# Relation features of each unit made inside the next unit of the expert mixture, in 64-row products of three passes

## The reference

```python
# layer 0, the mixture (8 experts, each with its batch norm _bn):
    h = jax.nn.relu(_bn(jnp.einsum('bfd,edh->bfeh', x, W1) + b1, g1, be1, m1, v1))
    h = jax.nn.relu(_bn(jnp.einsum('bfeh,ehk->bfek', h, W2) + b2, g2, be2, m2, v2))
    y = jnp.einsum('bfeh,ehd->bfed', h, Wo) + bo
    return jnp.einsum('bfed,fe->bfd', y, softmax(feat @ Wr + br))
# layer 1: xn = _layernorm(x), message (u->v) in relation r: norm_e * xn[u], then blockwise
    W = weight.reshape(R, NUM_BASES, SUBMAT_IN, SUBMAT_OUT)       # 8 relations, 8 blocks of 32x32
    out = jnp.einsum('rnbi,rbio->nbo', agg, W)
```

## Time and profile before

| | us |
|---|---|
| median of three runs | 7881.05 |
| the profiled execution | 7916.16 |
| its span | 7914.4 |
| TensorE busy | 5702.7 (72%) |
| VectorE busy | 4775.0 (60%) |
| ScalarE busy | 3998.3 (51%) |
| GpSimd busy | 3494.5 (44%) |

### The profile page before, as it was taken

How to read it: one execution, slowest core, us unless ns; L and a number is a source line. 1 busy time by engine, 2 the same in 40 slices (tenths; PEclk the granted TensorE clock), 3 DMA queues, 4 the chain that set the end, 5 groups by cost and what they waited for, 6 DMA issues and landing times. The chain is left out here.

```text
span 7914.4 us, 97807 instructions
## 1 busy us (share of the span) xinstructions
PE 5702.7 (72%) x22256; PEld 4016.0 (51%) x22256; DVE 4775.0 (60%) x13022; ACT 3998.3 (51%) x13304; POOL 3494.5 (44%) x3571
## 2 busy tenths in 40 slices
PE   3567777755677777547777777999987666666688
PEld 2434444434455555335555445888854555445445
DVE  5545555566555555855665557888843555656584
ACT  4456666665667766747677665444453111111032
POOL 2455566525656665266666660000002545556501
PEclk8767788776788888768888888999998777777799
DMA  5434444335333333343333333555575223222212
GB/s 164 124 104 111 111 118 113 110 89 151 100 98 104 102 100 98 108 137 101 101 103 100 100 99 119 200 188 192 192 238 194 85 86 90 85 81 80 71 41 66
DMA packets 511972, 920.50 MB, mean 116 GB/s; under 512 B 89659, under 2 KB 345611, under 8 KB 511435
## 3 DMA queue, kind: packets, MB, share of 16 engines
q0 software_dynamic: 166320, 446.82, 20.7%
q1 hardware_dynamic: 345259, 469.88, 18.4%
HBM read 773.29 MB, written 152.30 MB: 117 GB/s over the span
## 5 line engine op out<-in xcount | busy, mean ns | idle before, releaser
L1863 POOL DMA_INDIRECT gm_got<-scratch_feat,keep_src_tab x2490 | 2376.2, 954 | 1519.8 <-PE gm_bank L2141 678.1
L2141 PE MATMUL gm_bank<-gm_got,gm_onehot 128*128 128x264 f32 x4980 | 1886.2, 484 | 1013.9 <-DVE gat_acc L2023 482.6
L2085 ACT ACTIVATE gm_got<-gm_got 128x64 f32<-128x64 f32 x9804 | 2427.8, 334 | 271.4 <-issue 206.6
L2141 PEld LDWEIGHTS gm_bank<-gm_got,gm_onehot 128*128 128x128 f32 x4980 | 971.1, 226 | 1643.8 <-issue 793.5
L2023 DVE TENSOR_TENSOR gat_acc<-gat_acc,gm_bank 128x264 f32 x2490 | 1060.6, 426 | 1129.1 <-PE gm_bank L2141 512.1
L1151 POOL DMA_INDIRECT mix1a_got<-scratch_rel_feat,layer_rel_tab x240 | 238.9, 996 | 1483.6 <-issue 1359.0
L1151 POOL DMA_INDIRECT mix1b_got<-scratch_rel_feat,layer_rel_tab x590 | 588.3, 997 | 461.2 <-PE mix1b_m_bank L1208 234.0
L1208 PE MATMUL mix1b_m_bank<-mix1b_got,mix1b_onehot 128*128 128x256 f32 x1180 | 417.1, 498 | 311.3 <-DVE logit_acc L1182 249.4
L1208 PEld LDWEIGHTS mix1b_m_bank<-mix1b_got,mix1b_onehot 128*128 128x128 f32 x1180 | 269.4, 246 | 426.2 <-DVE mix1b_onehot L1160 213.2
L2030 DVE TENSOR_TENSOR gm_onehot<-gm_iota,keep_dst_tab 128x640 f32<-128x640 f32 x498 | 404.4, 812 | 73.9 <-issue 50.7
L850 POOL DMA_INDIRECT scratch_first<-gat_scores,keep_first_pos x150 | 200.8, 1339 | 507.5 <-DVE gat_scores L833 467.0
(11 more groups left out here) (579 smaller groups left out, 9873.4 us busy)
## 6 DMA issues: line engine op xcount, KB each, us to landing
moe_w<-scratch_ffn_cut SPq DMA_DIRECT2D x312, 512.0 KB, 3.4
scratch_rel_feat<-rel_out SPq DMA_DIRECT2D x50, 1024.0 KB
gm_got<-scratch_feat,keep_src_tab POOLq DMA_INDIRECT x2490
gm_flags<-scratch_flags SPq DMA_DIRECT2D x84, 300.0 KB
scratch_feat<-gf_row SPq DMA_DIRECT2D x50, 260.0 KB
gm_x<-scratch_x SPq DMA_DIRECT2D x50, 256.0 KB
gf_feat<-scratch_feat SPq DMA_DIRECT2D x50, 256.0 KB, 5.4
gf_old<-scratch_hidden SPq DMA_DIRECT2D x50, 256.0 KB, 4.2
```

What stands on the lines that cost most here:

```text
L1863: nc.gpsimd.indirect_dma_start(out=got[:, place // GROUPS, place % GROUPS * GROUP + j, 0:GAT_ROW], out_offset=None, in_=dram["feat"][layer ...
L2085: last = nc.scalar.activation(rows, rows, ACT.Copy, scale=got[:, b, i, D + h:D + h + 1])
L2141: nc.tensor.matmul(bank[i % BANKS][:, 0:GAT_SUM], onehot[:, i % HOTS, :], got[:, v[1] % B, i, :], start=True, stop=True).then_inc(s_sum, 1)
```

## The change

The relation features of the 48 tiles of the twelve full units are now made inside the mixture, each unit's during the unit that follows it. In that unit VectorE takes the statistics of the finished rows at its start (`rel_moments`), scales them in step 1 (`rel_rows`), and makes the low parts in step 3 (`rel_cut`); ScalarE makes the inverse root as exp(-0.5 ln(var + eps)) and copies out the transposes, which become the high parts (`rel_turned`); TensorE transposes at the end of step 2 (`rel_turn`) and in steps 3 to 6 makes two pieces a step (`rel_product`): a piece is one tile and one half of the features, three passes over two products of 64 rows by 512 columns, the one on the lower 64 rows into the bank `turn`, the other on the upper 64 into `route`. ScalarE evacuates each piece with two copies (`rel_half`) into one of three buffers, which lie in the part of the attention's accumulator that is used up, and SyncE stores it (0.5 MB in runs of 512 bytes; 1 KB before). The other two roots of a unit take the same form of exponential and logarithm, and VectorE's reciprocals behind them go; one set of ScalarE's tables is loaded ahead of the units. The first two units stand outside the loop now. `relation_features` keeps the last pair of tiles alone, without loops; it loads the other 48 tiles into `acc` with four DMAs, issued ahead of the pair's two stores, and its memset of the weights moves to GpSimd.

```diff
--- before.py
+++ after.py
@@ -2926,137 +2926,88 @@
 def relation_features(nc, io, dram, keep, acc, logit):
 
...
+    T = UNITS - 1
...
+                for k in range(4):
+                    rows = slice(k * 12, (k + 1) * 12)
+                    sp.dma_start(acc[:, rows, :], tiles[:, rows, :]).then_inc(s_acc, 16)
+                for i in range(PAIR):
+                    sp.wait_ge(s_out, len(pieces) // PAIR * (i + 1))
+                    sp.dma_start(to[:, T * PAIR + i, :, :], out[:, i, :, :]).then_inc(s_sent, 16)
                 sp.wait_ge(s_tab, 32)
+                sp.wait_ge(s_acc, 64)
+                sp.wait_ge(s_sent, 16 * PAIR)
...
+                def store_features(u, k):
+                    i, a = k // HALVES, k % HALVES
+                    sp.wait_ge(s_rel_out, rel_piece(u + 1, i, a))
+                    sp.dma_start(features[:, (u - 1) * QUAD + i, :, a * P:(a + 1) * P], rel_out[:, k % SLOTS, :, :]).then_inc(s_rel_sent[k % SLOTS], 16)
...
+                            if u > 0 and j and REL_AT <= e < REL_AT + QUAD:
+                                store_features(u, (e - REL_AT) * HALVES + j - 1)
                         if e == 2 and u > 0:
                             store(u - 1)
                             if u + 1 < N_U:
+                                sp.wait_ge(s_rel_x, u)
                                 load_x(u + 1)
+                        if e == REL_AT - 1 and u == 0:
+                            sp.wait_ge(s_rel_zero, 1)
+                            weight = io["L1_gnn_weight"].rearrange("r (b i o) -> b i r o", b=BLOCK, i=SUB)
+                            for b in range(BLOCK):
+                                lo, to = b % 4 * SUB, b % 2 * SUB
+                                sp.dma_start(w_whole[lo:lo + SUB, b // 4, :, to:to + SUB], weight[b]).then_inc(s_rel_w, 16)
                         if e == 3 and u + 2 < N_U:
...
                     c.done(last)
+                    dve.sem_inc(s_bias_read, 1)
+
+                def rel_moments(n, s):
+                    for i in range(QUAD):
+                        last = nc.vector.bn_stats(rel_stats[:, i, :], x[:, 1 - s, i, :])
+                    last.then_inc(s_rel_stats, 1)
+                    dve.wait_ge(s_rel_stats, n - 1)
+                    dve.sem_inc(s_rel_go, 1)
+                    for i in range(QUAD):
+                        last = nc.vector.bn_aggr(rel_mv[:, i, :], rel_stats[:, i, :])
+                    last.then_inc(s_rel_mv, 1)
+
+                def rel_rows(n, s):
+                    dve.wait_ge(s_rel_root, n - 1)
+                    for i in range(QUAD):
+                        last = nc.vector.tensor_scalar(rel_x[:, i, :], x[:, 1 - s, i, :], rel_mv[:, i, 0:1], rel_std[:, i:i + 1], ALU.subtract, ALU.mult)
+                    last.then_inc(s_rel_x, 1)
+
+                def rel_cut(n):
+                    dve.wait_ge(s_rel_high, n - 1)
+                    for i, bank in enumerate((bank_x, bank_g)):
+                        cols = slice(i * D, (i + 1) * D)
+                        last = low_part(rel_low[:, :, cols], bank[:, :].rearrange("p (a n) -> p a n", a=HALVES), rel_high[:, :, cols])
+                    last.then_inc(s_rel_xt, 1)
...
                     loaded = (n + 1) * 8 + 8 * s
                     gates(n, s, size)
+                    if rel:
+                        rel_moments(n, s)
+                    if rel and isinstance(n, int) and n == 2:
+                        dve.wait_ge(s_rel_w, 16 * BLOCK)
+                        high_part(rel_w[:, 0], w_whole).then_inc(s_rel_cut, 1)
+                        dve.wait_ge(s_rel_cut, 1)
+                        low_part(rel_w[:, 1], w_whole, rel_w[:, 0]).then_inc(s_rel_cut, 1)
                     for e in range(E + 2):
+                        if rel and e == REL_AT:
+                            rel_cut(n)
                         if e == E and after:
                             cut_rows(n + 1, after)
                         if e < E:
                             add_bias(n, s, size)
                         if 1 <= e <= E:
                             cut_layer(1, m + e, e - 1, size)
+                        if rel and e == 1:
+                            rel_rows(n, s)
                         if e >= 2:
                             gather_expert(m + (e - 1), s, e - 2, size)
                         if after:
...
                     act.wait_ge(s_std_in, n * 2)
-                    nc.scalar.activation(std[:, 0:size], mv[:, 0:size, 1], ACT.Sqrt, bias=keep["eps"][:, 0:1]).then_inc(s_std, 1)
+                    nc.scalar.activation(std[:, 0:size], mv[:, 0:size, 1], ACT.Ln, bias=keep["eps"][:, 0:1]).then_inc(s_log, 1)
+                    act.wait_ge(s_log, n)
...
+                def rel_turned(n):
+                    act.wait_ge(s_rel_t, n - 1)
+                    for i, bank in enumerate((bank_x, bank_g)):
+                        last = nc.scalar.copy(rel_high[:, :, i * D:(i + 1) * D], bank[:, :].rearrange("p (a n) -> p a n", a=HALVES))
+                    last.then_inc(s_rel_high, 1)
+
+                def rel_half(n, i, a):
+                    k = i * HALVES + a
+                    if k >= SLOTS or not isinstance(n, int) or n > 2:
+                        act.wait_ge(s_rel_sent[k % SLOTS], (n - 2) * (16 * SENT[k % SLOTS]) + 16 * (k // SLOTS))
+                    act.wait_ge(s_rel_mm, rel_piece(n, i, a))
+                    for q, bank in enumerate((bank_x, bank_g)):
+                        lo = q * 2 * SUB
+                        last = nc.scalar.copy(rel_out[:, k % SLOTS, :, lo:lo + 2 * SUB], bank[:, :].rearrange("p (r o) -> p r o", r=REL))
+                    last.then_inc(s_rel_out, 1)
 
                 def turned(n, size):
...
-                def unit(n, s, m, tile, size=QUAD, after=QUAD):
+                def rel_turn(n):
+                    pe.wait_ge(s_rel_x, n - 1)
+                    pe.wait_ge(s_bias_read, n)
+                    for i, bank in zip(range(0, QUAD, PAIR), (bank_x, bank_g)):
+                        last = transpose_pair(nc, bank, rel_x[:, i:i + PAIR], keep["ident"])
+                    last.then_inc(s_rel_t, 1)
+
+                def rel_product(n, i, a):
+
+                    if i == 0 and a == 0:
+                        pe.wait_ge(s_rel_xt, n - 1)
+                        if isinstance(n, int):
+                            pe.wait_ge(s_rel_cut, 2)
+                    else:
+                        pe.wait_ge(s_rel_out, rel_piece(n, i, a) - 1)
+                    passes = ((rel_high, 0), (rel_high, 1), (rel_low, 0))
+                    for k, (part, j) in enumerate(passes):
+                        for q, bank in enumerate((bank_x, bank_g)):
+                            rows = slice(q * 2 * SUB, (q + 1) * 2 * SUB)
+                            last = nc.tensor.matmul(bank[:, :], part[rows, a, i * P:(i + 1) * P], rel_w[rows, j, a, :, :].rearrange("p r o -> p (r o)"),
+                                                    start=(k == 0), stop=(k == len(passes) - 1))
+                    last.then_inc(s_rel_mm, 1)
+
+                def unit(n, s, m, tile, size=QUAD, after=QUAD, rel=True):
...
                             wide(bank1, 0, m, e, (xt_high, xt_low), size)
+                        if rel and REL_AT <= e < REL_AT + QUAD:
+                            rel_product(n, e - REL_AT, 0)
...
+                            rel_turn(n)
                         if e == E - 1 and after:
+                            if rel:
+                                pe.wait_ge(s_rel_out, rel_piece(n, QUAD - 1, HALVES - 1))
                             turn(n + 1, 1 - s, after)
```

More of the change, by code:

```diff
@@ L2959, in _ @@
             def _(sp):
+                sp.dma_start(acc[:, pair_tiles(T), :], tiles[:, pair_tiles(T), :]).then_inc(s_x, 16)
                 product.load_weight(sp)
[L2962 to L2977 removed]
                 sp.wait_ge(s_zero, 1)
@@ L2982, in _ @@
                     sp.dma_start(w[lo:lo + SUB, b // 4, :, lo:lo + SUB], weight[b]).then_inc(s_w, 16)
-                sp.sem_inc(s_free, UNROLL)
                 product.load_rest(sp)
-                part("load", (0, 1))
                 for n in ("rel_tab", "wt_tab"):
                     sp.dma_start(keep[n][:, :], dram[n]).then_inc(s_tab, 16)
-                with sp.Fori(0, ROUNDS - 2) as r:
-                    for name, ahead in (("store", 0), ("done", 0), ("load", 2)):
-                        part(name, (r, ahead))
@@ L3038, in _ @@
-                rounds(act, part, FIRST, BODY, LAST)
+                ln.root(nc, 0, 1)
+                act.wait_ge(s_xt, 1)
+                nc.scalar.copy(xt[:, :, :].rearrange("p a n -> p (a n)"), turned[:, :]).then_inc(s_xtc, 1)
+                for p, (i, a, g) in enumerate(pieces):
+                    act.wait_ge(s_mm, p + 1)
+                    nc.scalar.copy(out[:, i, 4 * g:4 * g + 4, a * P:(a + 1) * P],
+                                   bank[p % BANKS][:, :].rearrange("p (r o) -> p r o", r=4)).then_inc(s_out, 1)
```

(9 more changed lines are left out.)

151 lines of the change are left out of this document (69 added, 82 removed).

## The result

Ten runs of the changed kernel have a median of 7806.90 us (7780.91 to 7843.56), ten of the kernel before beside them 7892.89 (7853.43 to 7931.17): ratio 0.9902, 95% interval 0.9879 to 0.9925, so 77 us less (59 to 95). The forecast was 71 less and 7810. The profiled execution took 7780.91.

The account below looks back on a forecast made before the run. TensorE was taken to bound the mixture, VectorE close behind, DMA with room. Terms: 106 (units) + 2.6 + 1.9 (small edits) - 181 (relation stage) = -71 us, from a 7881.05 median to 7810; range 7775 to 7868.

Parts of the forecast that it names:

- Relation stage, -181: The relation stage shrinks from 228 us to a DMA queue of about 47 us, so 181 go (170 to 194).
- The pair side by side, 0.80 a piece: On TensorE in the mixture, two 64-row products run at once: 0.68 plus 0.12 us a piece, 6.4 a unit.
- Rival 1: On TensorE the 64-row products run one after another: 45 us more, 7855; chance 20%.
- Rival 2: On TensorE each change between whole and half rows empties the array, 0.35 us a change: 7865; chance 8%.
- Stalls: TensorE waits in a mixture unit for bias addition (1.4 us), low halves (1.3) and two roots (1.0 and 0.6).
- Rival 4: In the mixture, stalls one to three do not come: 50 us less, 7760; chance 10%.
- Given back, 2.7: TensorE's old waits in a mixture unit shrink: 1.6 us for VectorE's last gatings, 1.1 for evacuations.
- The unit, +8.9: Each full mixture unit grows 8.9 us from pieces, transposes and stalls, less time given back; eleven make 98.
- The last unit, +8: The last, short mixture unit grows 8 us, with the same pieces and about the same waits.
- Small edits: Table loads hidden, no gain; 2.6 us more ahead of the mixture loop, 1.9 for cutting the relation weights.
- DMA, 23 ns a packet: Mixture stores of 512 bytes cost between 23 and 47 ns, nearer 23; no cost in time.
- Rival 3: In mixture steps 3 to 6 the 512-byte stores bind, from 55 ns a packet; at 65 ns, 7971; chance 7%.

Follow-up runs that it names:

- one_pass: The changed kernel with one pass of the relation products instead of three, two matmuls a piece instead of six; ratio 0.9853 to the kernel before.
- full_rows: The changed kernel with its relation products run over all 128 rows instead of 64 each; ratio 0.9942 to the kernel before.
- stored_twice: The changed kernel with every store of relation features in the mixture issued a second time to an unread tensor; ratio 0.9956 to the kernel before.
- roots_alone: The kernel before with only the mixture's roots as exp(-0.5 ln), one table and no VectorE reciprocals; ratio 1.0013 to the kernel before.
- no_loop: The changed kernel with the mixture's looped units written out as calls; ratio 0.9885 to the kernel before.
- again: The changed kernel, unaltered, run once more on another chip for the spread; ratio 0.9905 to the kernel before.
- before_here: The kernel before, unaltered, profiled on the chip of the first follow-up runs, where it takes 6713 us.
- long_body: The kernel before with four already-met waits more in each product of six mixture matmuls, 256 instructions more in TensorE's loop body; ratio 1.0019 to the kernel before.

## Why the prediction was right, step by step

- **What bounds the unit.** Right. Less time in the products shortens the unit (one_pass), more lengthens it (full_rows).
- **Relation stage, -181.** It gave -190.3. The form was right (a queue, all else beside it; the pair takes 16 products and 7.1 us, not the 8 that I wrote, and they too are done beside it), with 39.9 us for my 46.7. (2.2 more of the 190.3 come from the measure, which takes the old stage up to 6037.2, not to VectorE's last operation.) The queue was filled by 5912.62, 9.5 us in and not 12.4, since the memset on GpSimd took 1.80, where I took 3, and the weights 3.8. What followed took 30.4 where I had 34.3: I priced it at the 271 GB/s of the earlier trace rows, but that was what the old stage asked for, at a share of 0.77. Left to itself the queue moved 355, and lost part of that again in the four slow us at its start.
- **The pair side by side, 0.80 a piece.** Right in kind; the size was short. The unstalled piece is 0.99 to the next layer's first product, and that one's slot is 0.11 too long: 1.10, so 8 x 0.30 = 2.4 a unit too little, 29 us in all. The 0.12 I gave for getting in and out measures 0.42. Rival 1 (1.36) is out by the start times and by full_rows. Rival 2 was right that a change costs something, and overstates it: 0.35 a change, two a piece, for the 0.42 measured.
- **Stalls.** All three came, smaller: bias 0.8 (1.4), low halves 1.0 (1.3), roots 0.5 where they show (1.6 for two). Together they are 2.3 a unit for the 4.3 of my sum. The removal of the first two gave 2.2 against 2.7. Rival 4 (no stalls) is out.
- **Given back, 2.7.** The wait for the gatings gave 1.4 (forecast 1.6). The 1.1 for evacuations came where the unit is looped: TensorE's waits for them were 9.6 us from 4870 to 5740, 7.3 of them behind the four back edges, and are gone. In written-out units, before too, there are none.
- **The unit, +8.9.** Written out it is 85.8 against 75.1: +10.7. With the measured terms my sum is 8.8 + 0.9 + 0.8 + 1.0 + 0.5 - 1.4 = 10.6 (the 0.9 for the transposes as forecast). The misses in the pieces (+2.4) and in the stalls (-2.0) went against each other, which was luck. The loop's 4 to 9 us were in no step of mine. One written-out unit of before and of after (columns of the earlier trace rows): busy +9.5, idle +1.2.

```profile
4818.90:4893.90 75.00, 72.65 (x422) 63.43 (x421) 63.47 (x111) 33.95 (x58) 0.00 (x0) 1.00 0.55 190
```
```profile
4903.30:4989.00 85.70, 82.19 (x476) 67.10 (x476) 68.13 (x123) 41.40 (x77) 0.00 (x0) 1.00 0.70 214
```

- **The last unit, +8.** It was +13.6. I gave it a full unit's TensorE price, but the DMA holds it up. Before, it had 45.5 us for the weights of a whole unit; 4.2 MB of stores at the 260 GB/s of its stretch are 16 us. A second set of stores there made it 12.5 us longer again (stored_twice). TensorE waits there for weights and ScalarE for slots (waits of 5844 to 5903):

```profile
ACT gat_acc L3493 <- DMA scratch_rel_feat<-gat_acc: 9.7, 4, 5.1
...
PE moe_third L3570 <- DMA moe_w<-scratch_ffn_cut: 3.8, 3, 1.7
```

- **Small edits.** Hidden table loads: right as far as roots_alone can tell. The 2.6 ahead of the loop did not come: the first period is 79.4 with 79.5 before, and what lies ahead of it is inside the spread. The 1.9 for the cut of the weights does not show either: its unit takes 85.7, as the others in no_loop.
- **DMA, 23 ns a packet.** Right, near the lower bound: in the packet records of the third to tenth period (again against before_here) a packet of 512 bytes takes 27 ns in the mean, one of 1 KB 52. The engines' time in a unit rose by more, 18 us (43.4 to 61.3) where 8192 x 27 ns on 16 engines are 13.8, for the weights' packets of 4 KB took 208 ns beside the stores instead of 191, and the rest I did not trace. Rival 3 needed 55, and even a second set of stores did not bind in whole units.
- **Sum.** Mixture +134 (forecast 106 + 1.9 for the cut), relation stage -190 (-181): -56 against -73 for the same stages. The mixture was under-priced by 26 and the relation stage's saving by 9. That the total, 7806.90, is so near 7810 is luck: by these stages the change was worth 17 us less than forecast, and the untouched stages and the run gave that back. Of the rivals none came as stated.

## What to carry to other kernels

Work hung into a loop has a price that no row of an engine's work shows: the length of the body. When a body grows, look at the branch at its end, at the first instruction of a turn on every engine for idle time put down to nothing, and at the granted clock behind it. A DMA rate read from a stage in which the queue was not the limit is no price for a stage in which it is (271 GB/s at a share of 0.77, and 355 once nothing else held the queue). And price a short last iteration by its own limit (here DMA bytes), not as a share of a full one.

## What the runs showed of the hardware

- Products on the lower and upper 64 rows start within 10 ns of each other, even with two others of the lower half between them in the program; a run of three such pairs among whole-row products costs 0.42 us over its three slots of 0.23 (0.31 up to the next product's start, 0.11 in that one's slot); six whole-row products in its place took 1.38, six slots of 0.23.
- Idle stretches of TensorE of 1.8 to 3.5 us at the back edge of a loop, behind a branch of 3.4 to 5.6 us, were followed by 3 to 10 us at half the clock (1.2 GHz), in all 25 of these traces (four in long_body, three in each of the seven traces of changed versions with the loop). The 2.3 us wait for the gatings in the kernel before is followed by the same only now and then: in 3 of its 11 the granted clock is 0.66 to 0.67 over the five us behind it, in the other 8 it stays 1.00. What decides it these runs do not show.
- A store packet of 512 bytes took 27 ns of a DMA engine and one of 1 KB 52, with the queue shared by 4 KB packets of 208.
